# State-space loop: the products of inputs and B rows for two states in one GpSimd operation

## The reference, cut to what matters

```python
def _selective_scan(u, delta, A, Bm, Cm, D):
    deltaA = jnp.exp(jnp.einsum('bld,dn->bldn', delta, A))
    dBu = delta[..., None] * Bm[:, :, None, :] * u[..., None]

    def step(state, inp):
        dA_t, dBu_t, C_t = inp
        state = dA_t * state + dBu_t
        y_t = jnp.einsum('bdn,bn->bd', state, C_t)
        return (state, y_t)
    ...
    return y + u * D
```

## Time and profile before

| what | value |
| --- | --- |
| median of 3 runs | 1975.6 us (1970.58 to 1976.54) |
| profiled execution, its own time | 1971.14 us |
| its span, first to last instruction | 1969.3 us |
| mean granted TensorE clock | 0.858 |
| the loop, first scan to last eviction | 720.8 to 966.7 us |

### The profile page before, as it was taken

The page is one execution under the profiler, slowest core; times in us unless marked ns, Lnnn a source line. Parts: engine busy times, 40 slices in busy tenths (PEclk is TensorE's granted clock), DMA queues, the critical chain, the costliest instruction groups (busy, mean ns, idle before and its releaser), DMA issues. The chain is left out here.

```text
span 1969.3 us, 23940 instructions
## 1 busy us (share of the span) xinstructions
PE 1465.7 (74%) x8427; PEld 1153.1 (59%) x8427; DVE 1427.8 (73%) x2337; ACT 810.7 (41%) x1552; POOL 593.0 (30%) x400
## 2 busy tenths in 40 slices
PE   3896323479999947767758951897778889779797
PEld 3574102369998423434448951884357789567697
DVE  7586677898665589999755745787976477675666
ACT  5475220465553755555214521762233243333332
POOL 1500002121220049999515224126212141100320
PEclk8997555889999978998868975899889989878899
DMA  4411000111101212240047511002343010320110
GB/s 97 110 28 44 1 0 0 52 50 43 44 1 39 89 52 67 69 129 8 24 153 175 150 57 44 22 17 40 111 122 86 21 45 11 77 31 2 41 33 26
DMA packets 65313, 108.76 MB, mean 55 GB/s; under 512 B 34750, under 2 KB 43549, under 8 KB 63583
## 3 DMA queue, kind: packets, MB, share of 16 engines
q1 hardware_dynamic: 57218, 92.96, 16.1%
q0 software_dynamic: 6416, 9.29, 2.3%
q10 hardware_dynamic: 1562, 5.00, 0.9%
HBM read 83.82 MB, written 18.13 MB: 52 GB/s over the span
## 5 line engine op out<-in xcount | busy, mean ns | idle before, releaser
L2535 POOL TENSOR_TENSOR c_dbub<-c_dub,s_bcb 128x814 f32<-128x814 f32 x96 | 169.4, 1785 | 84.5 <-DVE c_dub L2604 72.8
L2580 PE MATMUL c_pc<-c_st,ident 128*128 128x407 f32 x384 | 157.8, 560 | 48.4 <-POOL c_st L2543 41.7
L2519 ACT ACTIVATE c_da<-s_deltab,s_ab 128x407 f32<-128x407 f32 x192 | 108.1, 595 | 117.7 <-DVE c_st L2630 100.1
L2580 PEld LDWEIGHTS c_pc<-c_st,ident 128*128 128x128 f32 x384 | 77.4, 209 | 126.1 <-POOL c_st L2543 57.0
L2626 DVE TENSOR_TENSOR_SCAN c_da<-c_da,c_dbub 128x814 f32<-128x814 f32 x60 | 110.6, 1843 | 0.0
L2045 ACT ACTIVATE e_sg<-e_pu,e_b 128x444 f32<-128x444 f32 (+1 forms) x96 | 56.7, 591 | 80.3 <-PE e_pu L1971 74.8
L2126 DVE TENSOR_TENSOR e_sg<-e_sg,e_gate 128x444 f32<-128x444 f32 (+1 forms) x96 | 54.7, 570 | 48.4 <-ACT e_sg L2045 45.4
L3279 DVE SCALAR_TENSOR_TENSOR dc_acc<-dc_pp,dc_cw,dc_acc 128x1311 f32<-128x1311 f32 x48 | 75.9, 1584 | 17.8 <-ACT dc_acc L3212 16.0
L1933 POOL TENSOR_TENSOR e_wlb<-e_wb,e_whb 128x1024 fp32r<-128x1024 f32 x16 | 42.2, 2659 | 126.4 <-ACT e_whb L2020 126.4
L2814 POOL DMA_INDIRECT me_xe<-m_xs,mt_rowsb x48 | 47.9, 998 | 76.7 <-DVE mt_rowsb L2980 36.0
L2543 POOL TENSOR_TENSOR c_st<-c_st,s_bcb 128x814 f32<-128x814 f32 x36 | 68.6, 1905 | 4.6 <-DVE c_st L2623 4.6
(11 more groups left out here) (703 smaller groups left out, 4621.9 us busy)
## 6 DMA issues: line engine op xcount, KB each, us to landing
s_bcb<-s_bc SPq DMA_DIRECT2D x48, 407.0 KB, 4.0
m_wb<-in_m_w SPq DMA_DIRECT2D x16, 768.0 KB, 7.5
e_wb<-in_e_w SPq DMA_DIRECT2D x4, 2048.0 KB, 7.5
m_ys<-me_yb SPq DMA_DIRECT2D x16, 384.0 KB
d_z<-d_first ACTq DMA_DIRECT2D x11, 384.0 KB, 2.7
d_first<-d_z SPq DMA_DIRECT2D x11, 384.0 KB, 3.6
le_wb<-in_l_w_e SPq DMA_DIRECT2D x9, 384.0 KB, 3.1
de_wb<-in_d_w_e SPq DMA_DIRECT2D x8, 384.0 KB, 3.1
```

What stands on the lines that cost most here:

```text
L2519: last = nc.scalar.activation(da[k % 2][:, c * CH:(c + 1) * CH], delta[:, t, c0 + c, :], ACT.Exp, scale=a[:, n, c0 + c:c0 + c + 1])
L2535: nc.gpsimd.tensor_tensor(wide(dbu[k % DB][:, :]), du[:, t, c0:c0 + HC, :], bc[n][:, 0:1, :].broadcast_to([P, HC, CH]), ALU.mult).then_inc ...
L2580: last = nc.tensor.matmul(pc[:, c, 0:CH], ident[:, :], st[k % YB][:, c * CH:(c + 1) * CH], start=False, stop=(n == N - 1), skip_group_chec ...
```

## The change

GpSimd makes the products of steps k and k + 1 in one instruction, for even k. For this the 16 tiles of B and C rows become slices of one tile, and the four product buffers one tile of four rows, so that two neighbours can be addressed as one operand; du is read twice, with a stride of zero. The pair waits for both rows and for step k - 3, which read the second of its two buffers. c_dbu counts pairs, so VectorE and SyncE wait for k // 2 + 2. GpSimd's order becomes: the pair (0, 1) first; then, at each even k, the pair (k + 2, k + 3), and after it the C multiplications of k and of k + 1 where those steps are pooled.

```diff
@@ -2206,13 +2206,14 @@
         delta = sb("s_deltab", [P, NCH, C, CH])
         a = sb("s_ab", [P, N, C])
         dd = sb("s_db", [P, C])
-        bc = [sb(f"s_bcb{m}", [P, 2, CH]) for m in range(N)]
+        bc_all = sb("s_bcb", [P, N, 2, CH])
+        bc = [bc_all[:, m, :, :] for m in range(N)]
         w_out = sb("s_w_outb", [P, C, D])
         bc_dram = nc.dram_tensor("s_bc", (NCH, N, 2, CH), F32, kind="Internal").ap()
 
         def load(sp, t, m):
 
-            sp.dma_start(bc[m][:, :, :].rearrange("p m n -> p (m n)"),
+            sp.dma_start(bc[m].rearrange("p m n -> p (m n)"),
                          bc_dram[t, m:m + 1].rearrange("a m n -> a (m n)").broadcast_to([P, 2 * CH])
                          ).then_inc(sg[f"bc{m}"], 16)
 
@@ -2477,7 +2478,7 @@
             landed = [sg[f"bc{m}"] for m in range(N)]
             w_landed = sg["w_out"]
             du = sb2("c_dub", [P, NCH, C, CH])
-            dbu = [sb2(f"c_dbub{b}", [P, HW]) for b in range(DB)]
+            dbu = sb2("c_dbub", [P, DB, HW])
             st = [sb2(f"c_st{b}", [P, HW]) for b in range(YB)]
             dg = sb2("c_dgb", [P, C, P])
             zero = sb2("c_zerob", [P, HW // S])
@@ -2501,7 +2502,7 @@
                     for n in range(N):
 
                         k = (2 * t - 1) * N + n
-                        sp.wait_ge(s["c_dbu"], k + 2)
+                        sp.wait_ge(s["c_dbu"], k // 2 + 2)
                         if on_pool[n]:
                             sp.wait_ge(s["c_pool"], pooled[k + 1] + 1)
                         else:
@@ -2529,25 +2530,27 @@
                     u, n = at[k]
                     t, c0 = units[u]
                     pool.wait_ge(s["c_du"], t + 2)
-                    pool.wait_ge(landed[n], t * 16 + 16)
+                    for m in range(2):
+                        pool.wait_ge(landed[n + m], t * 16 + 16)
                     if k >= DB:
-                        pool.wait_ge(s["c_vec"], k - DB + 2)
-                    nc.gpsimd.tensor_tensor(wide(dbu[k % DB][:, :]), du[:, t, c0:c0 + HC, :],
-                                            bc[n][:, 0:1, :].broadcast_to([P, HC, CH]), ALU.mult
+                        pool.wait_ge(s["c_vec"], k - DB + 3)
+                    b = k % DB
+                    nc.gpsimd.tensor_tensor(dbu[:, b:b + 2, :].rearrange("p m (c n) -> p m c n", c=HC),
+                                            du[:, t, c0:c0 + HC, :].unsqueeze(1).broadcast_to([P, 2, HC, CH]),
+                                            bc_all[:, n:n + 2, 0:1, :].broadcast_to([P, 2, HC, CH]), ALU.mult
                                             ).then_inc(s["c_dbu"], 1)
 
                 def outputs(k):
                     n = at[k][1]
                     pool.wait_ge(s["c_vec"], k + 2)
                     one = wide(st[k % YB][:, :])
-                    nc.gpsimd.tensor_tensor(one, one, bc[n][:, 1:2, :].broadcast_to([P, HC, CH]), ALU.mult
+                    nc.gpsimd.tensor_tensor(one, one, bc_all[:, n, 1:2, :].broadcast_to([P, HC, CH]), ALU.mult
                                             ).then_inc(s["c_pool"], 1)
 
-                for k in range(DB - 1):
-                    inputs(k)
+                inputs(0)
                 for k, (u, n) in enumerate(at):
-                    if k + DB - 1 < K2:
-                        inputs(k + DB - 1)
+                    if k % 2 == 0 and k + 2 < K2:
+                        inputs(k + 2)
                     if on_pool[n]:
                         outputs(k)
 
@@ -2615,20 +2618,20 @@
                 for k, (u, n) in enumerate(at):
                     t, c0 = units[u]
                     dve.wait_ge(s["c_da"], k + 2)
-                    dve.wait_ge(s["c_dbu"], k + 2)
+                    dve.wait_ge(s["c_dbu"], k // 2 + 2)
                     if k >= YB:
                         dve.wait_ge(s["c_sum"], k - YB + 2)
                     da_k = da[k % 2][:, 0:HW]
                     if on_pool[n]:
-                        nc.vector.tensor_tensor_scan(st[k % YB][:, :], da_k, dbu[k % DB][:, :], 0.0, ALU.mult, ALU.add
+                        nc.vector.tensor_tensor_scan(st[k % YB][:, :], da_k, dbu[:, k % DB, :], 0.0, ALU.mult, ALU.add
                                                      ).then_inc(s["c_vec"], 1)
                     else:
-                        nc.vector.tensor_tensor_scan(da_k, da_k, dbu[k % DB][:, :], 0.0, ALU.mult, ALU.add
+                        nc.vector.tensor_tensor_scan(da_k, da_k, dbu[:, k % DB, :], 0.0, ALU.mult, ALU.add
                                                      ).then_inc(s["c_scan"], 1)
                         dve.wait_ge(s["c_scan"], k - pooled[k] + 2)
                         dve.wait_ge(landed[n], t * 16 + 16)
                         nc.vector.tensor_tensor(wide(st[k % YB][:, :]), wide(da_k),
-                                                bc[n][:, 1:2, :].broadcast_to([P, HC, CH]), ALU.mult
+                                                bc_all[:, n, 1:2, :].broadcast_to([P, HC, CH]), ALU.mult
                                                 ).then_inc(s["c_vec"], 1)
                     if k == 6:
                         moved_in(2)
```

## The result

The change makes the kernel slower, by about half a per cent. Beside the kernel before, in six executions each, the median is 1984.5 us against 1974.1, ratio 1.0058 (95% interval 1.0044 to 1.0072). Taken again on two chips the ratio is 1.0032 (1.0018 to 1.0046; 12 executions against 30) and 1.0051 (1.0035 to 1.0067; 6 against 11). Predicted was 1987, from 1979 to 1994.

The account below looks back on a forecast made before the run. VectorE was taken to set the loop's pace, GpSimd barely keeping up. Ten waits 9.7, moved_in(2) 1.6 and start 0.3 make +11.6 us, added to the median of 1975.6: 1987 us, range 1979 to 1994.

Parts of the forecast that it names:

- VectorE sets the pace, relief of GpSimd is worth nothing: Scan loop: VectorE sets the pace from first to last scan; time taken off GpSimd is worth nothing by itself.
- The wait at every multiple of 8, ten of them, from the order: At k = 16, 24, ..., 88 the scan waits for C multiplication then pair: 10 x 0.97 = 9.7 us.
- P: Duration of GpSimd's paired product of 1628 elements: 3.43 us, from 3.10 to 3.81; each wait is P - 2.46 us.
- moved_in(2): VectorE's multiplication at k = 6 waits for the running pair (8, 9): 4.28 us in place of 2.68, +1.6 us.
- The start: Before the first scan: two pairs have two ends in place of four, so the first scan comes 0.3 us later.
- A pair slower for each element: Rival on the GpSimd pair: P = 3.81, longer waits and four second waits, +18 us, 1994; chance 0.17.
- In time or faster: Two rivals: pair not slower and in time, 1976 us, chance 0.07; GpSimd's relief reaches the path, 1970 us, chance 0.03.

## Why the prediction was right

- **VectorE sets the pace, relief of GpSimd is worth nothing.** Shown: 9.8 us less on GpSimd, ratio 1.0002; the same with work taken off VectorE gives 0.9956.
- **The wait at every multiple of 8, ten of them, from the order.** Shown, at the predicted places. It goes when the C multiplication stands behind the pair, and it stays when the pair is two singles.
- **The size of a wait was mis-sized.** Predicted were 0.97 us each, measured is 6.96 - 6.32 = 0.64 us on the path (0.56 idle, the rest is overlap of neighbouring instructions that the wait breaks). P was 3.354 and not 3.43 us (-0.08). The larger part is the term that wasn't put in doubt: the C multiplication of 1.86 us from start to start became 1.58 (759.10 to 760.68) in the odd steps, -0.28, by the row's new address. With both, the prediction's own sum gives 1.92 + 1.58 + 3.35 + 0.08 - 6.32 = 0.61. With the rows padded it gives 0.89; measured 0.91.
- **moved_in(2).** Predicted +1.6 us, measured 742.46 - 738.52 = 3.94 in place of 2.68, +1.3. The pair (8, 9) started at 737.48, earlier than reckoned since the C multiplication ahead of it is shorter. moved_in(2) ended 1.71 us after the pair (742.54 against 740.83), where the prediction has 1.70. With two singles it took 2.38 us, so the cost is that of a long GpSimd instruction that holds VectorE's off to its end.
- **The start.** Predicted +0.3, measured 10.53 against 10.50 us from the first du to the first scan: nothing. Half of the 0.3 goes with the two shorter pairs.
- **The sum.** 10 x 0.64 + 1.3 = 7.7 us where 11.6 were forecast; the three comparisons make it 10 to 11, 6, and 10 to 11 us. What is missing to the 9.7 us of the first pair of profiles are waits for TensorE, 1.85 us in the profile after and 0.23 in the one before, and some hundredths of a microsecond in the step behind each wait. The prediction put TensorE at nothing because it asked only when VectorE wants a state buffer back, and not when the additions want their sums. These waits go with the granted clock, 0.2 to 3.4 us with single products in the old order, and are 0.9 to 1.9 in the changed kernel's three profiles. On the chip of the ratio 1.0032 the changed kernel's loop (0.9 us of them) is 5.6 us longer than that of single products (3.4 us of them), which is 0.0028 of the whole; that the kernel before had such waits there too is likely, but its profile was not taken on that chip. So a part of the agreement of 1987 with 1984.5 is luck: three terms, too large by 3.9 us together, stand against one left out. The 1987 also starts from a median of 1975.6, which with six executions is 1974.1. The 11 us behind the loop in the first profile stay unexplained; the median of the six, 10.5 us over that of before, doesn't need them.
- **The range.** The rival's terms at P = 3.81 add up to 18.3 us and not 18.4, and its start is too small: two pairs that are each 0.38 us longer end 0.76 later, so 1.1 and not 0.4. By the same step the start at P = 3.10 is -0.4 and not 0.1. The range would be 1978.5 to 1994.6, and nothing hangs on it.
- **The rivals.** A pair slower for each element: no, 3.354 us is 2.06 ns an element against 2.17. In time or faster: no.

## What to carry to other kernels

When an instruction is merged over two steps, look for what stands ahead of it in its queue at the step that now opens its gate, and add that to the path: here a scan (1.9 us with the hand-over), a C multiplication (1.6) and a pair (3.4) had to fit into 6.3 us. When two engines are nearly full, the waits tell which to relieve: here GpSimd, busy 96%, had waits and VectorE, at 99%, next to none. But relief of the other can be spent by moving work over from the one that sets the pace. And an edit that moves tiles can change the duration of instructions that it doesn't touch.

## What the runs showed of the hardware

The multiplication of 128x814 f32 by a broadcast row of 407 took GpSimd 1.90 us when the row started at 12 modulo 16 bytes (28 modulo 32 in the kernel before, 12 in the even steps after), and 1.63 us at 4 modulo 16. These offsets are worked out from the shapes in the program (a C row lies 1628 bytes behind its B row, a state 3256 bytes behind the one before) and take the tiles themselves to start at multiples of 32 bytes, which no trace shows. Padding made all 36 take 1.90 us, an 8-byte shift made all 36 take 1.63. Products, whose rows start at 0 or 8, kept to a median of 1.77 us in both layouts. That the effect is one of 16 bytes and not of 32 is argued from four offsets, not shown further.

A GpSimd product of 1628 elements took 3.354 us (3.336 to 3.369), against 3.50 us for two singles back to back: some 0.15 us saved.

GpSimd and VectorE held each other off in those operations of VectorE that read tiles of SBUF alone; the scans, which read the decay from PSUM, kept to 1.84 us beside it. VectorE's moved_in(2) took 4.02 us behind a pair, and one of the small scalings at the start 3.39 us; in the kernel before, one product of GpSimd took 3.38 us beside moved_in(2), where the median is 1.77.
